# Layer-0 attention start-up: weights in four loads, rotated stacks through scratch by fewer transfers, values' scale earlier

## The chip, the cores and the metric

One core of one Trainium2 chip runs the kernel. The metric is the device time of one execution in microseconds (us); the kernel before takes 1019.11 us, the median of three runs (1018.42 to 1019.32).

## The reference, cut to what matters

The program is two layers over x of shape (8, 512, 256). Layer 0 is `x + attention(norm(x)) + int8_ffn(norm(x))`, layer 1 is `x + gated_compare(norm(x)) + mix_ffn(norm(x))`. The change touches only the front of layer 0:

```python
xn = layernorm(x)
q = (xn @ Wq + bq).reshape(b, s, 16, 64)        # and k, v in the same way
q, k = rope(q), rope(k)                          # even and odd columns, cos and sin tables
scores = einsum('bnqd,bnkd->bnqk', q, k) / 8     # causal
attended = softmax(scores) @ v
```

Weights are scaled by a power of two taken from their largest absolute value, and each f32 operand is split in a high f16 and a low f16 part; products are three matmuls (high x high, high x low, low x high).

## The kernel before, in words

Every engine has a program written out by hand, and they meet on semaphores. The attention is a pipeline of "rings": ring n (from n = -5 to 62) does, for pair n of heads, the values, transposes and the product with the values, for pair n+1 the scores and the softmax, and for phase f = n + 5 (AHEAD = 5) the projection of queries (f even) or keys (f odd) of four heads. The helper `ring(n)` of each engine writes that order down; a stage of phase f goes through several rings:

- ring f - 5: PE makes the even and the odd columns (`evens`, `odds`, L1690), VectorE multiplies them with the tables (`even_terms` L1360 and L1362, `odd_terms` L1372 and L1373).
- ring f - 4: GpSimd (POOL) adds and subtracts the terms (`rotate`, L618 and L620), ScalarE (ACT) rounds to f16 (`high_e` L865, `high_o` L873), GpSimd makes the low parts (`low_e` L628, `low_o` L636). Each of the four results (hi_e, hi_o, lo_e, lo_o) is one tile of 128 partitions x 512 f16, single buffered: partition 32 h + r holds row r of head h.
- SyncE (SP) moves the four tiles to a scratch in DRAM and back, so that one head's 128 rows (hi even, hi odd, lo even, lo odd) lie on 128 partitions: `move_queries` (writes L494, reads L498) and `move_keys` (writes L508, reads L516, L517 into `kd`, which holds the high rows twice, and L519 into `kz`). A write waits for its tile to be made, a read for its piece of scratch to have landed (`sent`) and for the buffer to be free.
- PE's `scores` (L1761, L1762) waits for all of a quad's reads (`q_in`, `k_in`). The first is in ring -1. VectorE takes the row maxima (L1382), ACT the exponentials (L890), GpSimd normalises (L646).

Ahead of ring -5 VectorE takes the maximum of the query and key weights (L1239, two halves, each when its load has landed), `weight_scale` turns it into `inv`, ACT writes the high parts (L819, eight instructions, `halves`) and VectorE the low parts (`pairs_low`, L1228). ring -5's `evens` and `odds` wait for the low parts of the queries, ring -4's for those of the keys. In the gaps of rings -5 to -1 lie set-up steps: VectorE's `early` (maximum of the values' weights L1187, `row_sums` of batches 1 and 2, the scale) and `second_gap` (the values' low part, L1219, in ring -1), ACT's `later_weights` (statistics of batches 3 to 7 by `row_means` L790 and `row_squares` L800, the values' high part L808, w8 L845). PE fills its waits with matmuls that nobody reads (`fill`, `FILL`).

SP issues all loads in one queue, in the order of its program: x of batch 0, vec, the two halves of the query and key weights (L452), the tables, 16 tiny loads of the biases (L458), x of batches 3 and 4, the values' weights, x of 1, 5, 2, 6, 7, w8, thr, gate and the output weights (L468).

Of the kernel before, what the change touches and what calls it, by code (L numbers as in the profile page):

```python
# [16 lines left out]
NR = NB * NP  # L17
AHEAD = 5
NO = 12
EPS = 1e-5  # L20
MAGIC = 1.5 * 2.0 ** 23
MASKED = -1e30
# [21 lines left out]
def build(nc, x_d, weights_d, w8_d, bqk_d, vec_d, thr_d, gate_d, tab_d, out_d):  # L44
# [11 lines left out]
    with ctx:  # L56
        def sb(name, shape, dt):
            return ctx.enter_context(nc.sbuf_tensor(name, shape, dt))

        def sem(name):  # L60
            return ctx.enter_context(nc.semaphore(name))
# [27 lines left out]
        amax = sb("amax", [P, NB], f32)  # L89
        wmax = sb("wmax", [P, NG], f32)  # L90
        omax = sb("omax", [P, 4], f32)
        wqk_max = sb("wqk_max", [P, KT, 2], f32)
        wall = sb("wall", [P, NG], f32)
        sc = sb("sc", [P, NG], f32)
        inv = sb("inv", [P, NG], f32)
# [124 lines left out]


        x_loaded = [sem(f"x_loaded{b}") for b in range(NB)]
        wqk_loaded = [sem(f"wqk_loaded{k}") for k in range(KT)]
        fbo_set = sem("fbo_set")
        wv_loaded = sem("wv_loaded")
        wo_loaded = sem("wo_loaded")
# [215 lines left out]
        def _(sp):  # L442
# [4 lines left out]

            load_rows(0)
            sp.dma_start(vec[:], vec_d).then_inc(vec_loaded, 16)
            for k in range(KT):  # L450
                half = slice(k * C_V // KT, (k + 1) * C_V // KT)
                sp.dma_start(wst_qk[:, half], weights_d[:, half]).then_inc(wqk_loaded[k], 16)  # L452
            sp.dma_start(tabraw[:], tab_d).then_inc(tab_loaded, 16)
            b4 = bqk_d.rearrange("(q p c e r) -> r q p c e", q=NQ, p=2, c=4, e=2)
            for h in range(4):
                for a, c in ((0, 1 + h % 2), (1, 3 * (h % 2))):
                    for e in range(2):
                        sp.dma_start(bcol[h * HL:(h + 1) * HL, :, a, e], b4[:, :, h // 2, c, e],  # L458
                                     allow_slow_non_contiguous=True).then_inc(b_loaded, 16)
            load_rows(3)  # L460
            load_rows(4)
            sp.dma_start(wst_v, weights_d[:, C_V:C_O]).then_inc(wv_loaded, 16)
            for b in (1, 5, 2, 6, 7):
                load_rows(b)
            sp.dma_start(w8st, w8_d.bitcast(i32)).then_inc(c_loaded, 16)
# [12 lines left out]
            def fetch_columns(b):  # L478
# [5 lines left out]
                for c in range(2):  # L484
                    sp.dma_start(xs[u][c][:], xscr[b, c]).then_inc(x_in[u], 16)

            def move_queries(quad, par):

                f = 2 * quad
                after(sp, q_in[par], 64 * (quad // 2))  # L490
                for piece, tile, made_by, sent in ((0, hi_e, hie_done, hie_sent), (1, hi_o, hio_done, hio_sent),
                                                   (2, lo_e, loe_done, loe_sent), (3, lo_o, loo_done, loo_sent)):
                    sp.wait_ge(made_by, f + 1)
                    sp.dma_start(scr[par, 0, piece], tile).then_inc(sent, 16)  # L494
                after(sp, s_done, 12 * (quad - 1))
                for piece, sent in enumerate((hie_sent, hio_sent, loe_sent, loo_sent)):
                    sp.wait_ge(sent, 16 * (f + 1))
                    sp.dma_start(qs[par][piece * HL:(piece + 1) * HL],  # L498
                                 scr[par, 0, piece].rearrange("(h r) s -> r h s", h=4)).then_inc(q_in[par], 16)

            def move_keys(quad, par):

                f = 2 * quad + 1
                after(sp, k_in[par], 96 * (quad // 2))
                for piece, tile, made_by, sent in ((0, hi_e, hie_done, hie_sent), (1, hi_o, hio_done, hio_sent),
                                                   (2, lo_e, loe_done, loe_sent), (3, lo_o, loo_done, loo_sent)):
                    sp.wait_ge(made_by, f + 1)
                    sp.dma_start(scr[par, 1, piece], tile).then_inc(sent, 16)  # L508
                after(sp, s_done, 12 * (quad - 1))
                sp.wait_ge(kz_zero, 2)  # L510
                for piece, sent in enumerate((hie_sent, hio_sent, loe_sent, loo_sent)):
                    sp.wait_ge(sent, 16 * (f + 1))
                    rows = scr[par, 1, piece].rearrange("(h r) s -> r h s", h=4)
                    at = (piece % 2) * HL
                    if piece < 2:
                        sp.dma_start(kd[par][at:at + HL], rows).then_inc(k_in[par], 16)  # L516
                        sp.dma_start(kd[par][L + at:L + at + HL], rows).then_inc(k_in[par], 16)  # L517
                    else:
                        sp.dma_start(kz[par][at:at + HL], rows).then_inc(k_in[par], 16)  # L519

            def send_maxima(turn, src, count):

# [232 lines left out]
        def _(act):  # L755
# [79 lines left out]
            def later_weights(n):  # L835

                if n == -AHEAD:
                    row_sums(3)
                    row_sums(4)
                elif -AHEAD < n < 3 - AHEAD:  # L840
                    row_sums(n + AHEAD + 4)
                elif n == 3 - AHEAD:
                    row_means(7)
                    act.wait_ge(c_loaded, 16 * 3)
                    act.activation(w8[:], w8st.rearrange("p (k c w) -> p k c w", k=KT, w=2)[:, :, :, 0], ACT.Copy).then_inc(w8_done, 1)  # L845
                    act.wait_ge(setup_done, 2)
# [244 lines left out]
        def _(dve):  # L1091
# [140 lines left out]
            dve.memset(ones[:], 1.0).then_inc(ones_set, 1)  # L1232
            row_sums(0)
            inverse_roots(slice(0, 1), 0)
            for k in range(KT):
                dve.wait_ge(wqk_loaded[k], 16)
                for g in (G_Q, G_K):
                    half = staged(g)[:, k * 8:(k + 1) * 8]
                    last = dve.tensor_reduce(wqk_max[:, k, g - G_Q:g - G_Q + 1], half, AX.XYZ, ALU.max, apply_absolute_value=True)  # L1239
            link(dset, last)  # L1240
            dve.tensor_tensor(wmax[:, G_Q:G_V], wqk_max[:, 0], wqk_max[:, 1], ALU.max).then_inc(wmax_done, 2)
            over_partitions(2, 0)
            columns_low(0, 0)
            weight_scale(slice(G_Q, G_V), 0)
            columns_low(0, 1)
            dve.wait_ge(b_loaded, 16 * 16)
            for g in (G_Q, G_K):
                dve.tensor_scalar(bcol[:, :, g - G_Q], bcol[:, :, g - G_Q], inv[:, g:g + 1], None, ALU.mult)
# [42 lines left out]

            def second_gap(n):

                if n == -1:
                    weights_low(G_V, (wv_hi, 1), wv_lo)
                elif n == 0:
# [341 lines left out]
        def _(pe):  # L1638
# [473 lines left out]
```

## Time and profile before

| | us |
|---|---|
| median of the runs (lowest, highest) | 1019.11 (1018.42, 1019.32) |
| profiled execution, its own time | 1019.33 |
| its span | 1017.4 |
| PE busy in the span | 975.8 (96%) |
| DVE, ACT, POOL busy | 839.6, 746.0, 764.1 |
| granted clock of PE | 1.00 |

The span is 1.93 us shorter than the execution's own time; this stands for what lies around it. In the 40 slices of the page PE is at 5, 7 and 8 tenths in the first three and at 9 in nearly all of the others, so the stretch in which PE is not the bound is the first 60 us or so, which is where the change lies.

### The profile page before, as it was taken

The page shows a single profiled execution, that of the slowest core. Times are in us where ns is not written, and L with a number is a line of the kernel's source. Part 1 is how long each engine was busy: PE and PEld are TensorE (multiplying, and loading weights), DVE is VectorE, ACT ScalarE, POOL GpSimd, SP SyncE. Part 2 cuts the span into 40 slices and gives each one's busy share as a digit, 9 for nine tenths or more (in the row PEclk, how much of TensorE's full clock was granted, in tenths as well). Part 3 has the DMA queues.
Part 4 walks back from the last instruction along what each step waited for, and adds up shares of the span by engine and source line. Part 5 has one row for each costly group of instructions (what it writes and reads, how often), then busy time and mean ns, then how long its engine had stood idle before and what let it go on. Part 6 is the DMA issues. An engine that isn't in the chain of part 4 may idle for free.

```text
span 1017.4 us, 23654 instructions
## 1 busy us (share of the span) xinstructions
PE 975.8 (96%) x7956; PEld 673.2 (66%) x7956; DVE 839.6 (83%) x2272; ACT 746.0 (73%) x1998; POOL 764.1 (75%) x942
## 2 busy tenths in 40 slices
PE   5789999999999999999999999999999998989998
PEld 4556665766666666666666666666666675766776
DVE  7989999788889888887788777877878778999885
ACT  5989987667766677666767766667666776988984
POOL 3777768778778787878787878787878665878885
PEclk9999999999999999999999999999999999999999
DMA  8733535243433333333333333333333101111111
GB/s 271 242 111 119 155 121 160 79 131 112 124 111 93 105 106 94 95 114 96 93 95 119 96 103 97 116 97 100 105 96 95 53 1 27 35 35 35 48 55 43
DMA packets 102903, 101.32 MB, mean 100 GB/s; under 512 B 13952, under 2 KB 98560, under 8 KB 102144
## 3 DMA queue, kind: packets, MB, share of 16 engines
q1 hardware_dynamic: 102784, 99.81, 32.2%
q8 instruction: 65, 1.06, 0.5%
q14 instruction: 54, 0.44, 0.2%
HBM read 56.25 MB, written 40.90 MB: 95 GB/s over the span
## 4 chain that ended last, share of the span: by engine, by line
PE 70%; DVE 16%; ACT 4%; POOL 4%; issue 3%; DMA 2%; SPq 0%; DVEq 0%; POOLq 0%; ACTq 0%
PE bank L1690 23%; PE bank L1787 13%; PE bank L1773 12%; PE bank L1804 8%; PE bank L1761 6%; PE bank L1762 5%; DVE arena L1382 2%; POOL arena L646 2%; PE bank L1931 2%; DVE arena L1398 2%; ACT arena L890 1%; PE bank L1991 1%; DVE arena L1550 1%; DVE arena L1360 1%; DMA arena<-in_weights 1%
## 5 line engine op out<-in xcount | busy, mean ns | idle before, releaser
L646 POOL TENSOR_SCALAR arena<-arena,rc 128x128 f32<-128x128 f32 (+3 forms) x512 | 278.0, 560 | 176.5 <-DVE rc L1391 176.2
L890 ACT ACTIVATE arena<-arena,nm 128x256 f32<-128x256 f32 (+3 forms) x512 | 283.5, 554 | 109.0 <-DVE nm L1382 104.4
L1382 DVE CUSTOM_DVE_ANT_0 arena<-bank,mask_rows 128x256 f32<-128x256 f32 (+3 forms) x512 | 232.9, 483 | 89.0 <-PE bank L1762 83.9
L1773 PE MATMUL bank<-ident,arena 128*128 128x128 f32 x1280 | 211.8, 278 | 9.5 <-DVE arena L1398 4.4
L1773 PEld LDWEIGHTS bank<-ident,arena 128*128 128x128 f32 x1280 | 150.0, 141 | 68.4 <-DVE arena L1398 29.3
L1762 PE MATMUL bank<-arena 128*128 128x256 f16 (+3 forms) x512 | 152.9, 299 | 0.0
L1787 PE MATMUL bank<-arena 128*64 128x512 f32 (+3 forms) x1024 | 152.0, 439 | 0.0
L1761 PE MATMUL bank<-arena 128*128 128x256 f16 (+3 forms) x512 | 139.9, 300 | 2.0 <-DMA arena<-scr 2.0
L1787 PEld LDWEIGHTS bank<-arena 128*64 128x64 f32 x1024 | 67.8, 136 | 95.1 <-issue 70.6
L1398 DVE COPY arena<-bank 128x512 f32<-128x512 f32 (+3 forms) x256 | 124.5, 486 | 3.3 <-PE bank L1773 2.9
L898 ACT ACTIVATE arena<-bank 128x512 f32<-128x512 f32 (+3 forms) x256 | 108.3, 423 | 15.0 <-PE bank L1773 14.2
L1690 PE MATMUL bank<-xsh,wh 128*128 128x512 f16 x256 | 97.3, 380 | 3.1 <-DVE wl L1228 2.4
L1804 PE MATMUL bank<-wh,arena 128*128 128x256 f16 x512 | 99.7, 273 | 0.0
L1690 PE MATMUL bank<-xsl,wh 128*128 128x512 f16 x256 | 97.3, 380 | 0.0
L1690 PE MATMUL bank<-xsh,wl 128*128 128x512 f16 x256 | 97.3, 380 | 0.0
L890 ACT ACTIVATION_READ_ACCUMULATOR arena<-arena,nm 128x1 f32 x512 | 96.0, 187 | 0.0
L908 ACT ACTIVATE arena<-bank,bvs 128x512 f16<-128x512 f32 x64 | 44.0, 687 | 69.8 <-PE bank L1787 69.5
L1690 PE MATMUL bank<-wh,xsh 128*128 128x128 f16 x512 | 89.1, 219 | 1.6 <-DVE arena L1373 1.6
L1690 PE MATMUL bank<-wl,xsh 128*128 128x128 f16 x512 | 89.1, 219 | 0.0
L1690 PE MATMUL bank<-wh,xsl 128*128 128x128 f16 x512 | 89.1, 219 | 0.0
L618 POOL TENSOR_TENSOR arena<-arena 128x512 f32<-128x512 f32 x64 | 81.5, 1274 | 6.6 <-DVE arena L1373 6.5
L620 POOL TENSOR_TENSOR arena<-arena 128x512 f32<-128x512 f32 x64 | 83.0, 1296 | 0.0
(183 smaller groups left out, 2164.2 us busy)
## 6 DMA issues: line engine op xcount, KB each, us to landing
arena<-scr SPq DMA_DIRECT2D x320, 128.0 KB, 2.7
scr<-arena SPq DMA_DIRECT2D x256, 128.0 KB, 1.7
arena<-in_weights SPq DMA_DIRECT2D x5, 1024.0 KB, 7.5
x_sb<-in_x SPq DMA_DIRECT2D x8, 512.0 KB, 8.7
out<-x_sb SPq DMA_DIRECT2D x16, 256.0 KB, 2.2
xscr<-arena SPq DMA_DIRECT2D x12, 256.0 KB, 3.0
arena<-wh SPq DMA_DIRECT2D x40, 64.0 KB, 2.0
xsh<-xscr SPq DMA_DIRECT2D x6, 256.0 KB, 3.5
```

What stands on the lines that cost most here:

```text
L620: pool.tensor_tensor(r_o, t_es, t_oc, ALU.add).then_inc(r1_done, 1)
L646: last = pool.tensor_scalar(pr[slot][:, OFF[i]:OFF[i + 1]], pr[slot][:, OFF[i]:OFF[i + 1]], rc[:, slot, i:i + 1], 1.0, ALU.mult, ALU.mult)
L890: act.activation(pr[slot][:, OFF[i]:OFF[i + 1]], pr[slot][:, OFF[i]:OFF[i + 1]], ACT.Exp, scale=-1.0, bias=nm[:, slot, i:i + 1], accum_out ...
L898: act.activation(ptf[h][:, TOFF[j]:TOFF[j + 1]], (pt0, pt1)[h][:, 0:P * (NT - j)], ACT.Copy).then_inc(ptf_done[h], 1)
L1382: dve.tensor_tensor_reduce(pr[slot][:, OFF[i]:OFF[i + 1]], s_tile[i], mask_rows[:, SQ - P * (i + 1):SQ], -1.0, -MASKED, ALU.add, ALU.min, ...
L1398: dve.tensor_copy(ptf[1][:, TOFF[j]:TOFF[j + 1]], pt1[:, 0:P * (NT - j)]).then_inc(ptf_done[1], 1)
L1690: last = pe.matmul(out, lhs, rhs, start=(a == 0), stop=(a == len(pairs) - 1))
L1761: pe.matmul(out, q, kd[par][:, hh, 0:(i + 1) * P], start=True, stop=False)
L1762: last = pe.matmul(out, q, kz[par][:, hh, 0:(i + 1) * P], start=False, stop=True)
L1773: last = pe.transpose(banks[5 + h][:, (i - j) * P:(i - j + 1) * P], pr[2 * par + h][:, OFF[i] + j * P:OFF[i] + (j + 1) * P], ident[:])
L1787: last = pe.matmul(ob[h * L:(h + 1) * L, j * P:SQ], vf[:, j, h * L:(h + 1) * L], ptf[h][:, TOFF[j]:TOFF[j + 1]], start=(j == 0), stop=(j = ...
L1804: last = pe.matmul(bank[:, t * D:(t + 1) * D], o[:, slot, rows], w[:, p, :], start=(p == 0 and a == 0 and t == 0), stop=(p == NP - 1 and a ...
```

## The change

Query and key weights come in four loads of 512 KB instead of two of 1024 KB; their maxima are taken by quarter. The values' weights and x of batches 3 and 4 are issued ahead of the bias loads. The scratch holds each piece with row r of head h at row 4 r + h, so that the writes scatter (four groups of 32 rows) and the reads are contiguous; a quad's queries come back by one read instead of four, its keys by three instead of six. VectorE makes the keys' low parts ahead of ring -5's terms, scales the biases after them, and does the values' maximum, scale and low part about a ring sooner. ACT's statistics are split into means and squares around each ring's rounding. FILL's second entry goes from 60 to 24.

```diff
+NW = 4
-        wqk_max = sb("wqk_max", [P, KT, 2], f32)
+        wqk_max = sb("wqk_max", [P, NW, 2], f32)
@@ SyncE: loads
-            for k in range(KT):
-                half = slice(k * C_V // KT, (k + 1) * C_V // KT)
-                sp.dma_start(wst_qk[:, half], weights_d[:, half]).then_inc(wqk_loaded[k], 16)
+            for w in range(NW):
+                part = slice(w * C_V // NW, (w + 1) * C_V // NW)
+                sp.dma_start(wst_qk[:, part], weights_d[:, part]).then_inc(wqk_loaded[w], 16)
             sp.dma_start(tabraw[:], tab_d).then_inc(tab_loaded, 16)
+            load_rows(3)
+            sp.dma_start(wst_v, weights_d[:, C_V:C_O]).then_inc(wv_loaded, 16)
+            load_rows(4)
             b4 = bqk_d.rearrange("(q p c e r) -> r q p c e", q=NQ, p=2, c=4, e=2)
...
-            load_rows(3)
-            load_rows(4)
-            sp.dma_start(wst_v, weights_d[:, C_V:C_O]).then_inc(wv_loaded, 16)
@@ SyncE: stacks
+            def by_row(piece):
+                return piece.rearrange("(r h) s -> h r s", h=4)
+            def stacked(pieces):
+                return pieces.rearrange("c (r h) s -> (c r) h s", h=4)
             def move_queries(quad, par):
                 f = 2 * quad
-                after(sp, q_in[par], 64 * (quad // 2))
+                after(sp, q_in[par], 16 * (quad // 2))
...
                     sp.wait_ge(made_by, f + 1)
-                    sp.dma_start(scr[par, 0, piece], tile).then_inc(sent, 16)
+                    sp.dma_start(by_row(scr[par, 0, piece]), tile).then_inc(sent, 16)
                 after(sp, s_done, 12 * (quad - 1))
-                for piece, sent in enumerate((hie_sent, hio_sent, loe_sent, loo_sent)):
+                for sent in (hie_sent, hio_sent, loe_sent, loo_sent):
                     sp.wait_ge(sent, 16 * (f + 1))
-                    sp.dma_start(qs[par][piece * HL:(piece + 1) * HL],
-                                 scr[par, 0, piece].rearrange("(h r) s -> r h s", h=4)).then_inc(q_in[par], 16)
+                sp.dma_start(qs[par], stacked(scr[par, 0])).then_inc(q_in[par], 16)
             def move_keys(quad, par):
...
-                    sp.dma_start(scr[par, 1, piece], tile).then_inc(sent, 16)
+                    sp.dma_start(by_row(scr[par, 1, piece]), tile).then_inc(sent, 16)
                 after(sp, s_done, 12 * (quad - 1))
+                for sent in (hie_sent, hio_sent):
+                    sp.wait_ge(sent, 16 * (f + 1))
+                for rows in (slice(0, L), slice(L, P)):
+                    sp.dma_start(kd[par][rows], stacked(scr[par, 1, 0:2])).then_inc(k_in[par], 16)
                 sp.wait_ge(kz_zero, 2)
-                for piece, sent in enumerate((hie_sent, hio_sent, loe_sent, loo_sent)):
+                for sent in (loe_sent, loo_sent):
                     sp.wait_ge(sent, 16 * (f + 1))
...
+                sp.dma_start(kz[par][0:L], stacked(scr[par, 1, 2:4])).then_inc(k_in[par], 16)
@@ ScalarE: later_weights
                 if n == -AHEAD:
                     row_sums(3)
-                    row_sums(4)
-                elif -AHEAD < n < 3 - AHEAD:
-                    row_sums(n + AHEAD + 4)
+                    row_means(4)
+                elif n == 1 - AHEAD:
+                    row_squares(4)
+                    row_means(5)
+                elif n == 2 - AHEAD:
+                    row_squares(5)
+                    act.wait_ge(setup_done, 2)
+                    weights_high(G_V, wv_hi)
+                    row_means(6)
                 elif n == 3 - AHEAD:
+                    row_squares(6)
                     row_means(7)
...
-                    act.wait_ge(setup_done, 2)
-                    weights_high(G_V, wv_hi)
@@ VectorE
-            for k in range(KT):
-                dve.wait_ge(wqk_loaded[k], 16)
+            for w in range(NW):
+                dve.wait_ge(wqk_loaded[w], 16)
...
-            dve.tensor_tensor(wmax[:, G_Q:G_V], wqk_max[:, 0], wqk_max[:, 1], ALU.max).then_inc(wmax_done, 2)
+            dve.tensor_reduce(wmax[:, G_Q:G_V], wqk_max.rearrange("p w a -> p a w"), AX.X, ALU.max).then_inc(wmax_done, 2)
...
             columns_low(0, 1)
+            for g in (G_Q, G_K):
+                pairs_low(g, 0)
+                pairs_low(g, 1)
             dve.wait_ge(b_loaded, 16 * 16)
...
-            pairs_low(G_Q, 0)
-            pairs_low(G_Q, 1)
             def early(n):
                 if n == -AHEAD:
-                    pairs_low(G_K, 0)
-                    pairs_low(G_K, 1)
-                elif n == 1 - AHEAD:
                     dve.wait_ge(wv_loaded, 16)
                     weight_maximum(slice(G_V, G_O))
+                elif n == 1 - AHEAD:
                     row_sums(1)
+                    over_partitions(1, 1)
                 elif n == 2 - AHEAD:
-                    over_partitions(1, 1)
+                    weight_scale(slice(G_V, G_O), 1)
                     row_sums(2)
                 elif n == 3 - AHEAD:
-                    weight_scale(slice(G_V, G_O), 1)
+                    weights_low(G_V, (wv_hi, 1), wv_lo)
             def second_gap(n):
-                if n == -1:
-                    weights_low(G_V, (wv_hi, 1), wv_lo)
@@ PE
-                    pe.wait_ge(q_in[par], 64 * (n // 4 + 1))
-                    pe.wait_ge(k_in[par], 96 * (n // 4 + 1))
+                    pe.wait_ge(q_in[par], 16 * (n // 4 + 1))
+                    pe.wait_ge(k_in[par], 48 * (n // 4 + 1))
...
-            FILL = (0, 60, 0, 40)
+            FILL = (0, 24, 0, 40)
...
-                if n == 2 - AHEAD:
+                if n == 1 - AHEAD:
                     weight_maxima(slice(G_V, G_O), 1)
+                elif n == 2 - AHEAD:
+                    maxima_down(slice(G_V, G_O), 1)
                 elif n == 3 - AHEAD:
-                    maxima_down(slice(G_V, G_O), 1)
                     fill(30)
```

## Rows read from the trace of the kernel before

**Rows 1.** Busy time of each engine in stretches, with granted clock, DMA share, GB/s

```profile
30.00:40.00 10.00, 8.54 (x107) 4.55 (x106) 9.73 (x19) 9.62 (x41) 7.01 (x6) 1.00 0.75 252
200.00:800.00 600.00, 597.24 (x4919) 407.70 (x4918) 487.33 (x1434) 416.15 (x1171) 468.65 (x608) 1.00 0.35 105
```

**Rows 2.** Chain that ended last, 0 to 110 us: start, us, what

```profile
2.23 9.64 DMA arena<-in_weights
...
53.49 2.19 ACT arena L890 x8
```

**Rows 3.** Timeline of VectorE (parts of one row from narrower windows)

```profile
11.90 2.35 DVE L1239 TENSOR_REDUCE wqk_max<-arena 128x1 f32<-128x1024 f32 x2 [0.24 <-DMA arena<-in_weights]
...
17.48 0.36 DVE L1248 TENSOR_SCALAR bcol<-bcol,inv 128x8 f32<-128x8 f32 x2
17.75 4.48 DVE L1228 SCALAR_TENSOR_TENSOR wl<-arena,inv,wh 128x256 f16<-128x256 f32 x8
...
17.75 1.67 DVE L1228 SCALAR_TENSOR_TENSOR wl<-arena,inv,wh 128x256 f16<-128x256 f32 x2
...
20.96 1.26 DVE L1228 SCALAR_TENSOR_TENSOR wl<-arena,inv,wh 128x256 f16<-128x256 f32 x3
...
22.83 0.75 DVE L1360 SCALAR_TENSOR_TENSOR arena<-bank,bcol,cosq 128x512 f32<-128x512 f32 x1 [0.60 <-PE bank L1690]
...
25.47 5.27 DVE L1228 SCALAR_TENSOR_TENSOR wl<-arena,inv,wh 128x256 f16<-128x256 f32 x8
...
33.71 2.28 DVE L1187 TENSOR_REDUCE wmax<-arena 128x1 f32<-128x2048 f32 x1
...
46.53 0.42 DVE L1382 CUSTOM_DVE_ANT_0 arena<-bank,mask_rows 128x256 f32<-128x256 f32 x1 [0.86 <-PE bank L1762]
```

**Rows 4.** Timeline of ScalarE: start, us, engine, line, operation

```profile
16.88 5.01 ACT L819 ACTIVATE wh<-arena,inv 128x512 f16<-128x512 f32 x8 [3.42 <-DVE inv L1213]
...
26.07 0.40 ACT L790 ACTIVATE arena<-x_sb 128x256 f32<-128x256 f32 x1
...
28.03 0.51 ACT L800 ACTIVATE arena<-x_sb,nbx 128x256 f32<-128x256 f32 x1
...
36.45 0.63 ACT L873 ACTIVATE arena<-arena 128x512 f16<-128x512 f32 x1 [0.18 <-POOL arena L620]
...
41.83 0.63 ACT L865 ACTIVATE arena<-arena 128x512 f16<-128x512 f32 x1 [0.47 <-POOL arena L618]
43.06 0.63 ACT L873 ACTIVATE arena<-arena 128x512 f16<-128x512 f32 x1 [0.60 <-POOL arena L620]
...
47.87 0.49 ACT L890 ACTIVATE arena<-arena,nm 128x256 f32<-128x256 f32 x1
```

**Rows 5.** Timeline of GpSimd: start, us, engine, line, operation

```profile
33.92 1.27 POOL L618 TENSOR_TENSOR arena<-arena 128x512 f32<-128x512 f32 x1 [0.61 <-DVE arena L1373]
...
37.50 1.16 POOL L636 TENSOR_TENSOR arena<-arena 128x512 f16<-128x512 f32 x1
```

**Rows 6.** Timeline of SP's queue: start, us, what it issues

```profile
3.18 10.46 SPq L458 DMA_DIRECT2D bcol<-in_bqk  x16
...
34.99 1.75 SPq L498 DMA_DIRECT2D arena<-scr  x4
```

**Rows 7.** DMA: queue of the whole span, then issues: count, KB each, us to landing

```profile
q1 hardware_dynamic: 102784, 99.81, 32.2%
...
arena<-scr SPq DMA_DIRECT2D x320, 128.0 KB, 2.7
scr<-arena SPq DMA_DIRECT2D x256, 128.0 KB, 1.7
...
out<-x_sb SPq DMA_DIRECT2D x16, 256.0 KB, 2.2
```

**Rows 8.** DMA rate in 40 slices of 1.5 us, 0 to 60 us

```profile
GB/s 0 186 219 158 344 426 421 294 61 19 250 352 429 389 349 358 350 349 364 376 421 330 203 38 257 279 177 145 148 268 297 163 193 87 108 159 85 142 264 45
```

**Rows 9.** Timeline of PE: the first scores

```profile
45.99 0.27 PE L1761 MATMUL bank<-arena 128*128 128x256 f16 x1 [1.98 <-DMA arena<-scr]
```

More of the change, by code:

```diff
@@ L222, in build @@
         x_loaded = [sem(f"x_loaded{b}") for b in range(NB)]
-        wqk_loaded = [sem(f"wqk_loaded{k}") for k in range(KT)]
+        wqk_loaded = [sem(f"wqk_loaded{w}") for w in range(NW)]
         fbo_set = sem("fbo_set")
@@ L493, in move_queries @@
                     sp.wait_ge(made_by, f + 1)
-                    sp.dma_start(scr[par, 0, piece], tile).then_inc(sent, 16)
+                    sp.dma_start(by_row(scr[par, 0, piece]), tile).then_inc(sent, 16)
                 after(sp, s_done, 12 * (quad - 1))
-                for piece, sent in enumerate((hie_sent, hio_sent, loe_sent, loo_sent)):
+                for sent in (hie_sent, hio_sent, loe_sent, loo_sent):
                     sp.wait_ge(sent, 16 * (f + 1))
-                    sp.dma_start(qs[par][piece * HL:(piece + 1) * HL],
-                                 scr[par, 0, piece].rearrange("(h r) s -> r h s", h=4)).then_inc(q_in[par], 16)
+                sp.dma_start(qs[par], stacked(scr[par, 0])).then_inc(q_in[par], 16)
             def move_keys(quad, par):
                 f = 2 * quad + 1
-                after(sp, k_in[par], 96 * (quad // 2))
+                after(sp, k_in[par], 48 * (quad // 2))
                 for piece, tile, made_by, sent in ((0, hi_e, hie_done, hie_sent), (1, hi_o, hio_done, hio_sent),
@@ L507, in move_keys @@
                     sp.wait_ge(made_by, f + 1)
-                    sp.dma_start(scr[par, 1, piece], tile).then_inc(sent, 16)
+                    sp.dma_start(by_row(scr[par, 1, piece]), tile).then_inc(sent, 16)
                 after(sp, s_done, 12 * (quad - 1))
+                for sent in (hie_sent, hio_sent):
+                    sp.wait_ge(sent, 16 * (f + 1))
+                for rows in (slice(0, L), slice(L, P)):
+                    sp.dma_start(kd[par][rows], stacked(scr[par, 1, 0:2])).then_inc(k_in[par], 16)
                 sp.wait_ge(kz_zero, 2)
-                for piece, sent in enumerate((hie_sent, hio_sent, loe_sent, loo_sent)):
+                for sent in (loe_sent, loo_sent):
                     sp.wait_ge(sent, 16 * (f + 1))
[L513 to L519, printed above, removed]
+                sp.dma_start(kz[par][0:L], stacked(scr[par, 1, 2:4])).then_inc(k_in[par], 16)
             def send_maxima(turn, src, count):
@@ L1234, in _ @@
             inverse_roots(slice(0, 1), 0)
-            for k in range(KT):
-                dve.wait_ge(wqk_loaded[k], 16)
+            for w in range(NW):
+                dve.wait_ge(wqk_loaded[w], 16)
                 for g in (G_Q, G_K):
-                    half = staged(g)[:, k * 8:(k + 1) * 8]
-                    last = dve.tensor_reduce(wqk_max[:, k, g - G_Q:g - G_Q + 1], half, AX.XYZ, ALU.max, apply_absolute_value=True)
+                    part = staged(g)[:, w * 16 // NW:(w + 1) * 16 // NW]
+                    last = dve.tensor_reduce(wqk_max[:, w, g - G_Q:g - G_Q + 1], part, AX.XYZ, ALU.max, apply_absolute_value=True)
             link(dset, last)
-            dve.tensor_tensor(wmax[:, G_Q:G_V], wqk_max[:, 0], wqk_max[:, 1], ALU.max).then_inc(wmax_done, 2)
+            dve.tensor_reduce(wmax[:, G_Q:G_V], wqk_max.rearrange("p w a -> p a w"), AX.X, ALU.max).then_inc(wmax_done, 2)
             over_partitions(2, 0)
@@ L1245, in _ @@
             columns_low(0, 1)
+            for g in (G_Q, G_K):
+                pairs_low(g, 0)
+                pairs_low(g, 1)
             dve.wait_ge(b_loaded, 16 * 16)
             for g in (G_Q, G_K):
-                dve.tensor_scalar(bcol[:, :, g - G_Q], bcol[:, :, g - G_Q], inv[:, g:g + 1], None, ALU.mult)
-            pairs_low(G_Q, 0)
-            pairs_low(G_Q, 1)
+                last = dve.tensor_scalar(bcol[:, :, g - G_Q], bcol[:, :, g - G_Q], inv[:, g:g + 1], None, ALU.mult)
+            link(dset, last)
             def early(n):
                 if n == -AHEAD:
-                    pairs_low(G_K, 0)
-                    pairs_low(G_K, 1)
-                elif n == 1 - AHEAD:
                     dve.wait_ge(wv_loaded, 16)
                     weight_maximum(slice(G_V, G_O))
+                elif n == 1 - AHEAD:
                     row_sums(1)
+                    over_partitions(1, 1)
                 elif n == 2 - AHEAD:
-                    over_partitions(1, 1)
+                    weight_scale(slice(G_V, G_O), 1)
                     row_sums(2)
                 elif n == 3 - AHEAD:
-                    weight_scale(slice(G_V, G_O), 1)
+                    weights_low(G_V, (wv_hi, 1), wv_lo)
             def low_part(c):
@@ L1292, in second_gap @@
             def second_gap(n):
-                if n == -1:
-                    weights_low(G_V, (wv_hi, 1), wv_lo)
-                elif n == 0:
+                if n == 0:
                     roots(later_tiles, 1, (3,), wo)
```

## The prediction

> **What bounds the kernel now.** I first read the busy time by stretch. From 200 to 800 us PE is busy 597 of 600 us, and nothing in the change takes work from PE there; so only the start can move. From 30 to 40 us it is VectorE (9.73 of 10) and ACT (9.62) that are full [rows 1]. The chain of waits says how they join: it starts with the load of the weights, goes through VectorE's low parts, and in ring -1 it is on ACT, whose last exponentials of the ring end at 55.7 [rows 2]. The timelines of the engines show which wait ends last. PE's first scores start at 45.99, after 1.98 us of waiting for the keys' reads [rows 9], and their first maximum is taken at 46.53 [rows 3]; but ACT, which has been at its statistics and weights since 21.8, is free for the first exponential only at 47.87 [rows 4]. From there to 55.7 ACT has no gap. So the **start of ACT's first exponential** sets the end, and the keys' arrival lies some 0.9 us below it (46.95, when the first maximum ends, against 47.87). What the change does to the time is what it does to the later of these two.
>
> **Weights in four loads.** VectorE is free at 8.7, and the second half's two reduces run from 11.90 to 14.25, after the load lands at 11.87 [rows 2, 3]. A reduce of 1024 columns takes 1.13 us start to start (2.35 less the 0.09 of its tail, by two), of 2048 columns 2.19 (L1187); so 512 columns take 0.53 + 0.07 = 0.60. Eight of them are 4.8 us. The rate of the queue [rows 8] puts the quarters some 1.3 us apart, the first at about 8.0 and the last where the second half lands now. From 8.7 VectorE then runs nearly without waiting and is done at 13.55: **0.7 us sooner**. If the two more issues (0.45 us each) put the last quarter later by their 0.9, it lands at 12.8 and its two reduces end at 14.0: 0.2 sooner. That is the other bound. I take 0.7: the bytes ahead of it are the same, and each issue is done long before its data can move. The final reduce in place of a maximum costs nothing that shows. Everything up to `inv` and ACT's first high part moves with it, from 16.88 [rows 4] to 16.2.
>
> **Low parts first, biases after.** Now eight for the queries take 4.48 us, 0.83 apart for the first three and 0.39 for the last ones, and the eight for the keys 5.27 beside GpSimd's rotation [rows 3]. In the new order all sixteen follow each other from 16.9 (the first high part's end), three at 0.83 and thirteen at 0.39, since GpSimd idles then: done at 24.5. If the keys' eight keep their 5.27, 26.6; that is the other bound, and it would cost 2.1. The biases add 0.27. The terms of phase 0 so start at 24.8 instead of 22.83 [rows 3], take 2.64, and GpSimd begins phase 0 at 27.6 instead of 25.7. The bias loads have to land before 24.5: sixteen issues last 10.46 [rows 6] from 5.5 on, behind 2 MB at 350 to 430 GB/s [rows 8], so about 22; that cover is 2.5 us. PE, with 24 fills instead of 60, waits in both; its products are ready before VectorE in either case, so this is worth nothing, even if they ran at 1.2 GHz.
>
> **ACT's order.** ACT ends its eight high parts at 21.1, statistics of batch 3 (4.28) at 25.4 and means of batch 4 (1.9, 26.07 to 28.03 [rows 4]) at 27.3. `high_e` of phase 0 then waits for GpSimd's first result at 28.95: **1.7 us idle**, and `high_o` for the second 0.6 more. After that I walk both queues: phase 1's rotation runs at 32.35 instead of 33.92 [rows 5] (VectorE's terms follow the values' maximum, 2.2 us as in L1187 [rows 3]), phases 1 and 2 are ready when ACT comes to them, and ACT has no further gap. The same work stays ahead of the first exponential: 26.0 us from 21.8 to 47.87 less the 1.25 us of waits now there (0.18, 0.47, 0.60 [rows 4]) is 24.8. So ACT is free at 21.1 + 24.8 + 2.3 = 48.2: **+0.4 us**. The split moves the waits, it does not take them away. VectorE does the values' low part before ring -1 and is free at 44.4; that only uncovers slack.
>
> **The stacks.** Ten reads become four, and with them 2.6 us of SP's issuing go per quad (0.43 each); in no ring is SP on the chain. GpSimd finishes the keys' last low part now at 38.66 [rows 5], and PE starts 7.33 later. It would finish at 37.75, so with transfers as now the keys are there by 45.1, ACT's first maximum by 46.1, under 48.2. The contiguous reads change nothing that is waited for.
>
> The writes are another matter. Each is 128 rows of 1 KB, now to one contiguous block; all such transfers in the trace have 128 or 32 rows outermost, and 1.7 us is their median [rows 7]. The new destination is 4 groups of 32 rows, which no row of the trace has. **Bounds:** spread over all 16 DMA engines as before, it costs nothing; divided only by its outermost 4, four engines carry 32 rows each in place of 8, and the four writes of a phase queue up on the same ones: 96 rows more on each. A row costs 51 ns by the whole queue's share (32.2% of 16 x 1017.4 us over 102784 packets), 38 at the peak of 426 GB/s [rows 8], 62 by 256 KB against 128 KB (2.2 less 1.7 over 8 rows [rows 7]). I take division by four, since the outermost size is the only thing that every transfer of the trace has as a multiple of 16 and this one has not, and 45 ns, between the peak and the mean, as these engines have little else by then. Then:
>
> - Queries: the last landed by the fourth read's issue, 36.3 now [rows 6]; with its tile made 0.95 sooner and the loads ahead done sooner 35.0, plus 96 x 45 ns: 39.3. SP stands there, as it waits for all four ahead of the one read, and the keys' writes, made by 37.75, are queued behind it.
> - Keys: issued from 39.8, 1.3 fixed (1.7 less 8 rows), 1.2 for the query read ahead of them (8 rows of 4 KB), 128 x 45 ns = 5.8: 48.1. Their last read takes 2.7 [rows 7]: 50.8. PE to ACT is 1.0: the first exponential at **51.8 against 47.87, +3.9**. With 38 ns it is +2.3, with 62 ns +7.7. ACT's 48.2 is hidden below it.
>
> The Trainium skill ("DMA: Bandwidth & Descriptors", on why a DMA increments its semaphore by 16) says that the number of engines is the largest up to 16 that divides the slowest dimension of both sides; for 4 and 128 that is four. No transfer in this trace shows it, as all have multiples of 16. By that rule the sum is the +3.9 above, and without it the +0.4.
>
> In later rings the longer writes have room: a tile is made anew one ring (12.3 us) later, and PE waits for a read nowhere but at 45.99.
>
> **Sum.** 1019.33 (span 1017.4 plus 1.93) + 3.9 = 1023.2; the median lies 0.2 below the profiled execution: **1023.0 us**. 0.2% (2.0 us) is about what a measurement here can tell.
>
> **Rivals.**
> - *Writes over all 16 engines.* ACT's queue decides: 1019.1 + 0.4 = 1019.5. For it: the same bytes and rows. Against: the outermost 4. Its unknowns (up to 0.5 for the weights, 2.1 for the low parts) reach to 1022.1.
> - *Faster: ACT finds its rounding ready.* If GpSimd's phase 0 came 1.7 us sooner than I place it, ACT would lose nothing: 0.7 sooner and 1.25 of waits gone, 1017.1. That needs the writes on 16 engines too, and terms that begin before the sixteen low parts can be done at the measured pace. It ends on the other side of my forecast.
> - *The bias loads land after 24.5.* If their 16 issues stall behind the 2 MB put ahead of them, VectorE waits and each us beyond is one on ACT; a stall of 3 us gives 1022.5, if the writes cost nothing. It adds to no other case, since ACT is hidden below the keys.
> - *The split doesn't do what it says:* quarters that land together at 11.87 would leave 4.8 us of reduces, 2.4 later than now: 1022.6. The rate of the queue speaks against it.
>
> **Chances.** Writes on four engines 0.58, ending slower in nearly all (+2.3 at its cheapest); on sixteen with ACT's queue 0.30, no change; faster 0.07; late loads 0.05, mostly slower. Range: from 1018.2, inside the faster case, to 1026.8, where 62 ns per row would end. The likeliest case alone: 1021.3 to 1026.8. Faster 0.08, same 0.32, slower 0.60.
>
> **What would show it.** Right: the four writes of a phase land in 3 to 8 us rather than 1.7 to 4.3, the wait of PE's first scores for the reads grows to several us, and ACT idles ahead of its first exponential. ACT waits about 1.7 us ahead of phase 0's rounding. The second maximum (`inv`) comes 0.7 sooner. Wrong: writes that land in 1.7 us in mid-kernel, first scores by 45; then the time is ACT's.

## The result and the profile after

The changed kernel takes 1032.5 us (median of 4 runs, 1031.49 to 1034.28) against 1019.13 for the kernel before: a ratio of 1.0131, 95% interval 1.0117 to 1.0144, or 13.4 us more. The direction held, and at the start so did the mechanism, the slow writes. The size did not: 3.9 us were forecast, 1026.8 was the end of the range, and about a third of the loss came by a path that the forecast had ruled out.

The profiled execution took 1031.49 us, with a span of 1029.5, 12.1 us more than before. Busy time by stretch (columns as in [rows 1]) shows where:

```profile
30.00:40.00 10.00, 8.23 (x108) 4.85 (x108) 9.36 (x29) 8.81 (x33) 6.97 (x7) 1.00 0.45 165
40.00:50.00 10.00, 1.81 (x31) 1.64 (x29) 5.08 (x5) 7.89 (x29) 4.79 (x5) 0.79 0.53 157
50.00:60.00 10.00, 7.18 (x62) 4.78 (x63) 3.98 (x14) 6.87 (x25) 4.66 (x5) 0.70 0.28 79
...
120.00:140.00 20.00, 16.48 (x120) 10.04 (x122) 16.12 (x47) 16.11 (x45) 12.07 (x17) 1.00 0.36 114
200.00:800.00 600.00, 597.74 (x4905) 407.38 (x4904) 486.81 (x1430) 414.51 (x1166) 469.30 (x606) 1.00 0.35 103
```

From 40 to 50 us PE is nearly idle where it was busy 8.0 of 10 us, and its granted clock falls to 0.79 and 0.70. A second loss lies between 100 and 200 us, which the forecast did not have. From 200 us on nothing has changed.

The chain of waits of the changed kernel (start, us, what; the end of the set-up, ring -1 and the end of ring 0):

```profile
8.75 4.76 DVE wqk_max L1250 x8
...
16.89 4.69 DVE wl L1239 x9
...
24.63 0.29 DVE bcol L1262 x2
...
32.57 6.53 DMA scr<-arena
39.19 0.34 SPq L507
...
41.28 7.81 DMA scr<-arena
49.17 3.52 DMA arena<-scr
52.82 0.37 PE bank L1771
...
54.26 0.43 PE bank L1771
...
55.12 1.81 PE bank L1700 x6
56.93 2.23 PE bank L1677 x40
...
61.58 0.75 DVE arena L1382
...
71.30 0.33 PE bank L1783
```

The maxima of the weights now end at 13.5 and all sixteen low parts at 24.6: VectorE's part went as forecast (13.55 and 24.5). Then the chain is on the queries' writes (32.57 to 39.1), SP's one read, the keys' writes (to 49.1) and the last keys' read (3.5 us), until PE starts its first scores at 52.82 instead of 45.99 [rows 9]. L1677 are fill matmuls, whose result nobody reads.

SP's queue and PE's wait, in the timelines:

```profile
6.88 12.68 SPq L462 DMA_DIRECT2D bcol<-in_bqk  x16
19.60 2.63 SPq L447 DMA_DIRECT2D x_sb<-in_x  x5
...
29.77 3.30 SPq L503 DMA_DIRECT2D scr<-arena  x4
39.19 0.34 SPq L507 DMA_DIRECT2D arena<-scr  x1
39.57 2.31 SPq L516 DMA_DIRECT2D scr<-arena  x4
45.81 1.15 SPq L521 DMA_DIRECT2D arena<-scr  x2
49.17 0.45 SPq L525 DMA_DIRECT2D arena<-scr  x1
```

```profile
52.82 0.37 PE L1771 MATMUL bank<-arena 128*128 128x256 f16 x1 [11.01 <-DMA arena<-scr]
```

SP issues a read of the keys when their writes have landed. Two have at 45.81 and four at 49.17, so the last two took 3.36 us: 1.68 us each, or 52 ns per row if each of four engines carries 32 rows. Before, four reads of the queries were issued from 34.99 on [rows 6]; the one read now goes out at 39.19.

ACT's timeline up to the first exponential (the last bracket is the idle time before and its releaser):

```profile
29.12 0.63 ACT L876 ACTIVATE arena<-arena 128x512 f16<-128x512 f32 x1 [1.88 <-POOL arena L624]
...
53.91 0.51 ACT L901 ACTIVATE arena<-arena,nm 128x256 f32<-128x256 f32 x1 [2.78 <-DVE nm L1392]
```

Further on it shows the second loss, in rings 3 to 6. L773 is `columns_high`, which waits until the columns of the batch before are stored to scratch:

```profile
105.52 0.60 ACT L773 ACTIVATE arena<-bank 128x512 f16<-128x512 f32 x1 [0.44 <-DMA xscr<-arena]
...
119.47 0.60 ACT L773 ACTIVATE arena<-bank 128x512 f16<-128x512 f32 x1 [1.48 <-DMA xscr<-arena]
...
134.07 0.60 ACT L773 ACTIVATE arena<-bank 128x512 f16<-128x512 f32 x1 [2.11 <-DMA xscr<-arena]
...
146.79 0.60 ACT L773 ACTIVATE arena<-bank 128x512 f16<-128x512 f32 x1 [0.23 <-DMA xscr<-arena]
```

The chain shows how such a wait arises (ring 5): the slow writes, then SP's read that waits for them, then the store of the columns behind it on SP, then ACT.

```profile
121.86 6.73 DMA scr<-arena
...
128.66 0.32 SPq L507
...
129.03 0.43 SPq L475
...
129.50 4.49 DMA xscr<-arena
...
134.07 0.61 ACT arena L773
```

From these rows the 12.1 us of the span fall in three parts. The first exponential moves from 47.87 to 53.91: **6.0 us**. A transpose of PE near the end of ring 0, at 71.30 in the chain above, was in the chain of before at

```profile
63.49 0.33 PE bank L1773
```

It comes 7.8 us later, so **1.8 us** more were lost in rings -1 and 0. There the chain changes its engine: it ran on ACT before and now runs on PE and VectorE. PE takes 8.6 us from its first scores to those of ring 0 (52.82 to 61.38) instead of 7.0 (45.99 to 52.98), as scores of 512 columns take 0.43 us instead of 0.21 and the six products behind them 1.81 instead of 1.3, at the lower clock. The 40 fills of ring -1 (2.23 us) lay beside ACT's work before and are now in the chain. ACT's last exponential of the ring starts 6.8 us later than before (61.66 against 54.87), 1.0 less than the chain lost, so by an estimate from these rows about 1 us would come back without the fills; no run took them out. The rest, **4.3 us**, is the columns' stores; ACT's four waits above are 4.26.

### The profile page after: what moved, and what is told of

Its sections match the earlier page's. It is cut to its first block, busy times and chain, and to the rows that moved or that the text cites. A ratio compares the mean times of both kernels' runs of the same rounds, so it can differ in the third digit from the quotient of the medians.

```text
span 1029.5 us, 23463 instructions
## 1 busy us (share of the span) xinstructions
PE 974.2 (95%) x7920; PEld 671.2 (65%) x7920; DVE 838.3 (81%) x2276; ACT 747.2 (73%) x1998; POOL 763.5 (74%) x942
## 4 chain that ended last, share of the span: by engine, by line
PE 68%; DVE 14%; DMA 5%; POOL 5%; ACT 4%; issue 4%; SPq 1%; POOLq 0%; DVEq 0%; ACTq 0%
PE bank L1700 22%; PE bank L1797 12%; PE bank L1783 12%; PE bank L1814 8%; PE bank L1771 6%; PE bank L1772 5%; DMA scr<-arena 3%; DVE arena L1392 2%; PE bank L1942 2%; POOL arena L652 2%; DMA xscr<-arena 1%; DVE arena L1408 1%; PE bank L2002 1%; DVE arena L1560 1%; ACT arena L901 1%
## 5 line engine op out<-in xcount | busy, mean ns | idle before, releaser
L1783 PE MATMUL bank<-ident,arena 128*128 128x128 f32 x1280 | 211.7, 278 | 13.5 <-ACT arena L909 6.2
L624 POOL TENSOR_TENSOR arena<-arena 128x512 f32<-128x512 f32 x64 | 81.5, 1273 | 6.9 <-DVE arena L1383 6.9
L634 POOL TENSOR_TENSOR arena<-arena 128x512 f16<-128x512 f32 x64 | 74.4, 1162 | 12.3 <-DMA scr<-arena 12.3
```

What stands on the lines that cost most here:

```text
L624: pool.tensor_tensor(r_e, t_ec, t_os, ALU.subtract).then_inc(r0_done, 1)
L1783: last = pe.transpose(banks[5 + h][:, (i - j) * P:(i - j + 1) * P], pr[2 * par + h][:, OFF[i] + j * P:OFF[i] + (j + 1) * P], ident[:])
```

## The experiments

The short names: "old transfers" are the scratch layout, writes and reads of the kernel before. Each run was timed beside the kernel before on its own chip, so ratios are compared.

**Old transfers in the changed kernel.**

```diff
-                    sp.dma_start(by_row(scr[par, 0, piece]), tile).then_inc(sent, 16)
+                    sp.dma_start(scr[par, 0, piece], tile).then_inc(sent, 16)
...
-                sp.dma_start(qs[par], stacked(scr[par, 0])).then_inc(q_in[par], 16)
+                    sp.dma_start(qs[par][piece * HL:(piece + 1) * HL],
+                                 scr[par, 0, piece].rearrange("(h r) s -> r h s", h=4)).then_inc(q_in[par], 16)
```

> The changed kernel with the scratch layout, the four writes and the four and six reads of the kernel before; loads, VectorE's, ACT's and PE's orders stay as changed. Theory (the whole loss is in the writes on few DMA engines): the first scores start at 45.1 or sooner, ACT's first exponential at 48.2, time 1019.5, between 1018.5 and 1020.5. Rival (the new order of the set-up costs by itself, as the loads or ACT's waits fall badly): 1022 or more, with a gap on ACT or VectorE before 48 us that is over 3 us.

Measured: 1021.65 us, ratio 1.0020 (1.0009 to 1.0030). Eleven of the thirteen us go with the transfers, but 2 us stay, and both expectations missed: ACT has no large gap, yet the keys come late (first scores at 47.79, where 45.1 was expected). The chain and PE's timeline of this run:

```profile
29.79 6.64 DMA scr<-arena
36.45 0.32 SPq L499
```

```profile
47.79 0.37 PE L1766 MATMUL bank<-arena 128*128 128x256 f16 x1 [5.95 <-DMA arena<-scr]
```

The queries' first write is issued at 29.79 and landed only at 36.4. The DMA rate in 40 slices of 1.5 us of this run says why:

```profile
GB/s 0 171 296 317 339 391 419 380 410 402 311 70 7 7 248 357 337 345 367 391 336 390 305 53 38 253 171 183 139 248 219 187 130 208 239 210 208 277 127 0
```

From 16.5 to 21 us the queue moves 70, 7 and 7 GB/s. The idle stretch that lay from 12 to 15 us [rows 8] was not filled; it moved behind the three loads put first, since SP is in the 16 bias issues until 19.8 and x of the other batches stands behind them. Those loads then run until about 34, ahead of the queries' writes.

**Old transfers and old load order.**

```diff
-            load_rows(3)
-            sp.dma_start(wst_v, weights_d[:, C_V:C_O]).then_inc(wv_loaded, 16)
-            load_rows(4)
             b4 = bqk_d.rearrange("(q p c e r) -> r q p c e", q=NQ, p=2, c=4, e=2)
...
+            load_rows(3)
+            load_rows(4)
+            sp.dma_start(wst_v, weights_d[:, C_V:C_O]).then_inc(wv_loaded, 16)
             for b in (1, 5, 2, 6, 7):
```

> The run with the old transfers of the stacks, and on top the loads in the order of the kernel before (16 bias loads right behind the tables, then x of batches 3 and 4 and the values' weights); the weights still come in four. Theory (the new load order leaves the DMA queue empty from 16 to 21 us, because SP stands in the bias loads until 19.8, so the last loads and behind them the queries' writes land later): x of batch 1 is issued by 16.5, the first query read at about 35 instead of 36.5, first scores at 46, time 1019 to 1020, 1 to 2 us less than that run. Rival (the load order is worth nothing, the 2 us are ACT's new waits and PE's clock): 1021 to 1022.

Measured: 1019.2 us, ratio 1.0001 (0.9992 to 1.0010). The load order was worth the 2 us: the medians of the two runs are 2.4 us apart, though their intervals just touch, and the first scores start 2.8 us sooner. What is left of the change (weights by quarter, low parts first, ACT's split, values sooner) is worth nothing that this interval, 1 us to either side, would show. PE's and ACT's timelines:

```profile
45.02 0.27 PE L1766 MATMUL bank<-arena 128*128 128x256 f16 x1 [3.22 <-DMA arena<-scr]
```

```profile
29.10 0.63 ACT L871 ACTIVATE arena<-arena 128x512 f16<-128x512 f32 x1 [1.88 <-POOL arena L619]
30.33 0.63 ACT L879 ACTIVATE arena<-arena 128x512 f16<-128x512 f32 x1 [0.60 <-POOL arena L621]
...
47.80 0.49 ACT L896 ACTIVATE arena<-arena,nm 128x256 f32<-128x256 f32 x1
```

These are the rows of the forecast's other branch, nearly to the number: ACT idle for 1.88 and 0.60 us (1.7 and 0.6 forecast), keys there at 45.02 (45.1), first exponential at 47.80 (48.2). But the forecast gave them for the changed kernel's own load order, and with that (the run before this one) the keys came at 47.79 and the time was 1021.65 us, not 1019.5.

**The kernel before, with 4 outermost in its writes, and a control.** The scratch's four blocks of 32 rows are set a row apart; reads, waits and everything else are those of before. In the control each row is set apart instead, which leaves 128 outermost.

```diff
-        scr = nc.dram_tensor("scr", (2, 2, 4, P, SQ), f16).ap()
+        scr = nc.dram_tensor("scr", (2, 2, 4, 4, 33, SQ), f16).ap()
-                    sp.dma_start(scr[par, 0, piece], tile).then_inc(sent, 16)
+                    sp.dma_start(scr[par, 0, piece, :, 0:32, :], tile).then_inc(sent, 16)
```

> The kernel before, with a scratch whose four blocks of 32 rows are set one row apart, so that a write has 4 outermost but its rows stay in order, and all reads and waits stay. Theory (number of engines by the outermost dimension): writes take as long as in the changed kernel (a phase's four done 8 us after the first issue), GpSimd waits for them ahead of L636, time 1028 to 1034. Rival (it is the scattered addresses, or the one wait for all four writes on SP, that costs): as before, 1018.4 to 1020.

```diff
+        scr = nc.dram_tensor("scr", (2, 2, 4, P, SQ + 128), f16).ap()[..., 0:SQ]
```

> Control for the run with the four blocks set apart: the kernel before with every scratch row set apart (a pitch of 640 instead of 512 elements), so that 128 stays outermost but nothing is one block. Theory (number of engines): as before, 1018.4 to 1020, writes landing in 1.7 us. Rival (a write that isn't one block is slow): near 1028.

Measured: 1028.65 us, ratio 1.0095 (1.0080 to 1.0110), and for the control 1019.16 us, ratio 1.0000 (0.9989 to 1.0011). SP's timeline of the first, with old reads that wait piece by piece, against the control's:

```profile
40.21 2.24 SPq L508 DMA_DIRECT2D scr<-arena  x4
44.05 0.31 SPq L516 DMA_DIRECT2D arena<-scr  x1
...
45.67 0.30 SPq L516 DMA_DIRECT2D arena<-scr  x1
...
47.38 2.58 SPq L519 DMA_DIRECT2D arena<-scr  x2
```

```profile
36.48 2.67 SPq L508 DMA_DIRECT2D scr<-arena  x4
39.27 1.02 SPq L516 DMA_DIRECT2D arena<-scr  x1
```

The four pieces land some 1.7 us behind one another (44.05, 45.67, 47.38), as in the changed kernel; in the control they keep up with SP. So the outermost size alone costs 9.5 us, with addresses in order and single reads. The old transfers gave 11 us back; what is between the two (scattered addresses, one read behind four writes, or noise, as the intervals meet) was not taken apart.

**Each scattered write cut by head,** 32 rows outermost.

```diff
-                    sp.dma_start(by_row(scr[par, 0, piece]), tile).then_inc(sent, 16)
+                    for h in range(4):
+                        sp.dma_start(by_row(scr[par, 0, piece])[h], tile[h * HL:(h + 1) * HL]).then_inc(sent, 16)
```

> The changed kernel, each scattered write cut in four writes of one head's 32 rows, so that 32 is outermost; the scattered addresses, the contiguous reads and SP's wait for all writes stay. SP issues 16 writes per phase, some 7 us at 0.43 each. Theory (number of engines): landing in 2 to 3 us each, no wait of GpSimd for the scratch over 1 us, first scores by 48 us, time 1019.5 to 1022.5. Rival (scattered addresses or the single wait cost): 1030 or more.

Measured: 1039.54 us, ratio 1.0196 (1.0181 to 1.0212). The theory missed, with first scores at 54.80 instead of 48; the number is in the rival's range, but for another cause. The issues and SP's timeline:

```profile
scr<-arena SPq DMA_DIRECT2D x1024, 32.0 KB, 1.6
```

```profile
29.80 8.36 SPq L504 DMA_DIRECT2D scr<-arena  x16
40.90 0.34 SPq L508 DMA_DIRECT2D arena<-scr  x1
41.28 7.38 SPq L518 DMA_DIRECT2D scr<-arena  x16
```

Each write lands in 1.6 us, but 16 issues fill SP for 7.4 to 8.4 us per phase, and ACT's waits for the columns' stores grow to 4.69 us at 138: by these rows SP took the place of the DMA engines. The run says that 32 scattered rows in a write of their own land fast, and nothing about scattered addresses in one transfer with 32 or 128 outermost; that was not tried.

**A second set of result tiles** for the phases up to 19. My reading of GpSimd's 12.3 us of waits for scratch writes was that the single tiles carry the loss behind 80 us.

```diff
-        hi_e, hi_o, lo_e, lo_o = (carve(SQ, f16) for _ in range(4))
+        hi_e, hi_o, lo_e, lo_o = ([carve(SQ, f16), wh[:, C_LR + i * SQ:C_LR + (i + 1) * SQ]] for i in range(4))
...
+        def before_last(f):
+            return 16 * (f - 1) if f < 20 else 16 * f
...
-                after(pool, loe_sent, 16 * f)
+                after(pool, loe_sent, before_last(f))
```

> The changed kernel with a second set of the four result tiles for the phases up to 19, so that ACT and GpSimd wait for the writes of two phases before instead of those of the last. Theory (the slow writes cost twice: once through the keys' late arrival, once through the single tiles, some 5 us of PE's waits between 80 and 200 us): the first scores still start near 50 to 53 us, PE's waits behind ACT L909 from 80 to 200 us go, 1026 to 1029. Rival (all of it is the late arrival): 1031.5 to 1033.

Measured: 1031.99 us, ratio 1.0128 (1.0114 to 1.0142). That theory fell: GpSimd's waits for the writes went, the time stayed. (Its first scores came at 54.04, 1.2 us later than in the changed kernel, so a gain of that size elsewhere is not ruled out.) ACT still waited for the columns' stores (1.13 us at 108, 2.79 us at 136), and this pointed to SP's order.

**Stores of the columns ahead of SP's wait for the four writes** (shown for the queries; the same in `move_keys`).

```diff
+                store_columns(2 * quad - 4)
                 after(sp, s_done, 12 * (quad - 1))
                 for sent in (hie_sent, hio_sent, loe_sent, loo_sent):
...
                 move_queries(quad, quad % 2)
-                store_columns(2 * quad - 4)
```

> The changed kernel with SP's stores of the columns (xscr) issued before it waits for a phase's four writes, not behind it. Theory (the second part of the loss, some 4 us between 95 and 160 us, is ACT L773 waiting for column stores that stand on SP behind the wait for the slow writes): ACT's waits for xscr (0.4, 1.5, 2.1 us) go, the first scores stay at 52 to 53 us, 1028 to 1029.5. Rival (those stores wait in the DMA engines, not on SP, or the loss there is of another cause): 1031.5 to 1033.

Measured: 1027.22 us, ratio 1.0080 (1.0067 to 1.0093), 0.0051 below the changed kernel, or 5 us, a little more than was expected. ACT has no wait for xscr left, while the first scores stay at 52.11. The second part of the loss is shown: the store stands in SP's queue behind a wait for slow writes, and ACT's next column product waits for it.

**Old load order in the changed kernel,** the same edit as above.

> The changed kernel with the loads in the order of the kernel before (weights still in four). Theory (load order and slow writes add up): 2.4 us less than the changed kernel, 1029.5 to 1031, the first query read at about 37 instead of 39.2. Rival (behind the slow writes the load order is hidden): 1032 to 1033.

Measured: 1030.57 us, ratio 1.0117 (1.0104 to 1.0131). It lies where the sum of the two was expected, but the intervals meet, so this alone shows no gain. Its query read goes out at 38.25, 0.9 sooner, and the first scores at 51.48, 1.3 sooner.

**PE's clock.** 190 fills instead of 30 in ring -2 of the changed kernel:

```diff
-                    fill(30)
+                    fill(190)
```

> The changed kernel with 190 fill matmuls instead of 30 in ring -2, 8.9 us more at 0.055 each, inside PE's 11.0 us wait for the keys. Theory (the granted clock of 0.79 and 0.70 from 40 to 60 us is a part of the loss, some 2 us: scores at 0.43 us per 512 columns and six products in 1.81 us): 1030.0 to 1031.3. Rival (the clock costs nothing as ACT and GpSimd bound there): 1032 to 1033.

Measured: 1031.46 us, ratio 1.0120 (1.0101 to 1.0138). The granted clock of 40 to 50 us rises from 0.79 to 1.00 and of 50 to 60 from 0.70 to 0.83; the gain, about 1 us, is within the intervals, and the time lies between the two expectations. The clock was not wholly given back: in this profile the six products behind the first scores still take 2.56 us.

```diff
-            FILL = (0, 24, 0, 40)
+            FILL = (0, 60, 0, 40)
-                    fill(30)
+                    fill(70)
```

> The run with the old transfers and the old load order, with 60 fills back in ring -4 and 70 instead of 30 in ring -2 (2.2 us more inside PE's wait for the first keys). Theory (the granted clock falls in that wait and the first scores and products then run at 1.2 GHz): granted clock 1.00 from 40 to 50 us, 0.5 to 1.5 us less than the run without. Rival (ACT bounds there): the same within 0.3 us.

Measured: 1019.19 us, ratio 1.0003 (0.9994 to 1.0013), as without. There ACT sets the first exponential, and the rival holds.

**ACT's statistics regrouped** (with old transfers and load order), then with the fills above.

```diff
                     row_sums(3)
-                    row_means(4)
+                    row_sums(4)
                 elif n == 1 - AHEAD:
-                    row_squares(4)
-                    row_means(5)
+                    row_sums(5)
                 elif n == 2 - AHEAD:
-                    row_squares(5)
+                    row_means(6)
                     act.wait_ge(setup_done, 2)
                     weights_high(G_V, wv_hi)
-                    row_means(6)
```

> The run with the old transfers and the old load order, with ACT's statistics regrouped: batch 4 whole in ring -5, batch 5 whole in ring -4, means of batch 6 ahead of the values' high part in ring -3. Theory (the split as changed leaves ACT idle for 1.9 and 0.6 us ahead of phase 0's rounding, and ACT sets the first exponential at 47.8 while the keys' scores are there at 45.0): both waits are filled, ACT's first exponential starts at 45.9 to 46.2, time 1017.2 to 1017.8. Rival (the later rounding of phase 0 delays the keys as much as ACT gains): 1019.

> The run with ACT's statistics regrouped, and with 60 fills in ring -4 and 70 in ring -2. That run's profile has a granted clock of 0.69 from 40 to 50 us, scores of 512 columns at 0.43 us and the six products behind them in 2.56 us; two of its twelve executions took 1017.3, the others 1019.5 to 1021. Theory (what ACT gained was given back by PE's clock, which falls in PE's wait for the keys): granted clock 1.00 from 40 to 50 us, all executions near 1017.3. Rival (the clock in that wait is worth nothing, the keys or ACT bound): 1019 to 1020.5 as before.

Measured: 1020.41 us, ratio 1.0007 (0.9998 to 1.0015), then 1018.5 us, ratio 0.9993 (0.9983 to 1.0002). The timelines and the stretch of 40 to 50 us, of the first and of the second:

```profile
46.57 0.51 ACT L894 ACTIVATE arena<-arena,nm 128x256 f32<-128x256 f32 x1
```

```profile
40.00:50.00 10.00, 6.23 (x45) 3.51 (x43) 6.58 (x13) 8.98 (x32) 8.81 (x7) 0.69 0.65 195
```

```profile
46.18 0.49 ACT L894 ACTIVATE arena<-arena,nm 128x256 f32<-128x256 f32 x1
```

```profile
40.00:50.00 10.00, 8.95 (x129) 7.68 (x128) 8.67 (x16) 9.35 (x33) 9.26 (x7) 1.00 0.67 202
```

The first run missed both expectations: ACT is ready 1.2 us sooner, and the time is 1.4 us above even the rival's 1019. In its profile the chain is on PE, with first scores of 512 columns at 0.43 us, six products in 2.56 and the 40 fills of ring -1 in 2.41. With the clock at 1.00 in the second, ACT is ready 1.6 us sooner and the median is 1.9 us lower, but the two intervals overlap, so the clock as the cause is likely and not shown; that all executions would be near 1017.3 did not come true. In the second run the profiled span is 1015.6, 1.8 us under that of before, but the runs reach from 1016.83 to 1021.17 and the interval holds 1: no version was shown to beat the kernel before.

## Why the prediction was right and wrong

**Right.** The writes with 4 outermost set the keys' arrival: 4 outermost alone costs 9.5 us in the kernel before, and a copy with 128 outermost costs nothing. The Trainium skill ("DMA: Bandwidth & Descriptors", on why a DMA increments its semaphore by 16) gives four engines for these sizes. The pacing of 1.7 us per write agrees with 32 rows on one engine each; no row of a trace here counts the engines. VectorE's part was right (13.5 and 24.6 against 13.55 and 24.5), and so was ACT's wait ahead of its rounding (1.88 us against 1.7). The branch without slow writes was right only with the loads in their old order.

**The term mis-sized: the price of the writes and of the read behind them.** The queries were landed at 39.2 as written (39.3), but about 1 us of that agreement is luck: the loads ahead were done later, not sooner, and with the loads in their old order it is 38.2. Behind that the sum had 48.1 for the keys' last write and 50.8 for their read; measured 49.1 and 52.7. A row costs 52 ns, not 45. The last read took 3.5 us, not 2.7: the sum took the median of a read of 128 KB [rows 7], and this one moves 256 KB. So the first exponential was 6.0 us late instead of 3.9.

**The step that failed: "In later rings the longer writes have room".** I looked at who waits for the reads and who writes the tile again, and not at what else stands in SP's queue behind the new wait for all four writes. There stand the columns' stores, and ACT waits for them: 4.3 us in the profile, 5 us by the run that moved them. The tiles had no room either: GpSimd waited 12.3 us for the writes ahead of L634, in three waits, but in the run with two sets of tiles the time was the same.

**A term left out: PE's clock.** I priced PE's clock at nothing beside the fills of ring -4 and did not carry my own forecast further: a wait that grows from 2 to 11 us comes with a granted clock of 0.7 to 0.8, and with the chain now on PE, the first scores and products at 1.2 GHz cost 1.6 of the 1.8 us lost there. That PE's own fills of ring -1 would come to lie in the chain was not forecast either. Refilling the wait got back about 1 us, within the intervals.

**A sign that was wrong: "the loads ahead done sooner".** They were done later. Sixteen bias issues took 12.7 us, not 10.5, and the loads behind them start at 19.6 instead of 15.3. That cost 2.4 us in the run with old transfers; in the changed kernel's profiles it is 0.9 us on the query read and 1.3 on the first scores, and its time does not show it. The biases themselves were no wait: VectorE went from the low parts to them without a gap, so that cover held.

The parts make the 12.1 us of the spans: 6.0 late keys (about 1 of it by the load order), 1.8 in rings -1 and 0 (mostly the clock), 4.3 columns.

## What to carry to other kernels

When a transfer's layout changes, look at the outermost size on both sides: one of 4 made writes of 128 KB follow each other at 1.7 us where 128 made no queue. When a wait on a queue grows, list everything issued behind it on that queue, to the last store, and who waits for each. When a wait ahead of an engine grows, look at what that engine does behind it that cost nothing while another was the bound, such as fills. Here loads put ahead of a long row of small issues did not fill the queue; they moved the hole behind them.

## What the runs showed of the hardware that was not expected

Sixteen issues of 128 pieces of 4 bytes each took 10.5 us of SP when 3 MB were queued ahead, and 12.2 to 13.3 us when 2 MB more were; with the same 3 MB but the weights in four loads they took 8.2 to 9.3 us. Sixteen issues of 32 KB took 7.4 to 8.4 us. Contiguous reads of 4 KB per partition (512 KB in 3.2 us, 256 KB in 4.1 us at the median, behind slow writes) brought nothing that a wait here shows (no run has them without the slow writes), though the packets of the whole kernel fell from 102903 to 66325. Two of the twelve executions with ACT regrouped ended 3 us under the others, at the same order of instructions.
